# One graph layer on one core: first stage worked tile by tile, neighbour sums dealt out over other steps, feed-forward stage in another order

## What is computed

```
xn = layernorm(x)
# graph part: relation products, mean over the incoming edges, gate
u = xn @ root + bias
for r in range(8):
    sums = segment_sum(xn[src] * (edge_type == r), dst)
    u = u + (sums / max(count, 1)) @ weight[r]
z = concatenate([u, xn]) @ w_gate + b_gate
gnn = tanh(u) * z + xn * (1 - z)
# mix part: rms norm, q, k, v of 8 heads of 16, Taylor attention, w_out
x = x + gnn + mix(xn)
# feed-forward part: FP4 quantize-dequantize of rows and weights, 352 hidden
x = x + fp4_linear(silu(fp4_linear(ln(x), w_gate)) * fp4_linear(ln(x), w_up), w_down)
```

## Time and profile before

| | us |
|---|---|
| median of 3 runs | 1644.76 (1642.74 to 1646.51) |
| the profiled execution, its own time | 1644.54 |
| its span in the trace | 1642.8 |
| PE busy | 1554.4 |
| DVE, POOL, ACT busy | 890.7, 809.8, 406.0 |

### The profile page before, as it was taken

One profiled execution on the slowest core, in us unless ns is written; L12 is line 12 of the kernel. 1 busy time (PEld: TensorE's weight loads), 2 busy tenths in 40 slices (PEclk: granted clock), 3 DMA queues, 4 the chain that ended last, 5 costly groups with the idle time before them and its releaser, 6 DMA issues.

```text
span 1642.8 us, 19045 instructions
## 1 busy us (share of the span) xinstructions
PE 1554.4 (95%) x7138; PEld 1259.3 (77%) x7138; DVE 890.7 (54%) x1334; ACT 406.0 (25%) x595; POOL 809.8 (49%) x682
## 2 busy tenths in 40 slices
PE   4999999999999999999999999999999879997988
PEld 4987777777778678888887888888777758876887
DVE  6535222444442320003888888884667656877785
ACT  3321112222222112122222222222211123232320
POOL 4426766667663136545555565654655634232220
PEclk9999999999999999999999999999999989998999
DMA  4422323333333222226777788877889874540001
GB/s 160 144 89 80 92 79 94 108 98 102 95 90 112 71 78 99 84 88 222 263 254 255 245 276 281 278 242 240 301 285 317 287 257 163 186 148 0 39 39 49
DMA packets 120459, 262.48 MB, mean 160 GB/s; under 512 B 23451, under 2 KB 37010, under 8 KB 120360
## 3 DMA queue, kind: packets, MB, share of 16 engines
q1 hardware_dynamic: 48568, 109.34, 19.9%
q0 software_dynamic: 33056, 83.02, 16.6%
q10 hardware_dynamic: 38736, 68.83, 11.3%
HBM read 193.33 MB, written 80.06 MB: 166 GB/s over the span
## 4 chain that ended last, share of the span: by engine, by line
PE 63%; DVE 16%; issue 8%; DMA 6%; POOL 3%; ACT 2%; ACTq 0%; POOLq 0%; SPq 0%; DVEq 0%
PE ps L1831 49%; DMA source_rows<-relation_rows,row_list 6%; PE ps L2074 5%; PE ps L2083 2%; DVE u_sum L1580 2%; PE ps L1958 1%; PE ps L1914 1%; PE ps L1938 1%; PE ps L1950 1%; POOL source_rows L922 1%; POOL xf L1025 1%; DVE u_sum L1590 1%; ACT source_rows_hi L2292 1%; PE ps L2144 1%; DVE xf L1726 1%
## 5 line engine op out<-in xcount | busy, mean ns | idle before, releaser
L1831 PE MATMUL ps<-WH,XTH 128*128 128x512 f32 (+1 forms) x1680 | 666.9, 397 | 0.0
L1831 PE MATMUL ps<-WH,XTL 128*128 128x512 f32 (+1 forms) x1680 | 652.6, 388 | 0.0
L1831 PE MATMUL ps<-WL,XTH 128*128 128x512 f32 (+1 forms) x1680 | 652.5, 388 | 0.0
L864 POOL TENSOR_TENSOR WL<-RAW,WH 128x512 fp32r<-128x512 f32 (+1 forms) x184 | 243.6, 1327 | 289.4 <-ACT WH L2210 286.4
L1831 PEld LDWEIGHTS ps<-WH,XTH 128*128 128x128 f32 x1680 | 318.4, 190 | 65.6 <-issue 7.1
L1831 PEld LDWEIGHTS ps<-WH,XTL 128*128 128x128 f32 x1680 | 316.7, 189 | 64.8
L1831 PEld LDWEIGHTS ps<-WL,XTH 128*128 128x128 f32 x1680 | 317.6, 189 | 60.7 <-issue 2.4
L922 POOL DMA_INDIRECT source_rows<-relation_rows,row_list x180 | 221.6, 1231 | 235.4 <-DVE u_sum L1580 130.7
L2232 ACT ACTIVATE EV<-ps 128x512 f32<-128x512 f32 x180 | 107.6, 598 | 631.6 <-PE ps L1831 543.2
L943 POOL DMA_INDIRECT edge_lists<-edge_words x160 | 196.9, 1231 | 46.4 <-issue 44.2
L1580 DVE SCALAR_TENSOR_TENSOR u_sum<-source_rows,weight_list,u_sum 128x1024 f32<-128x1024 f32 x120 | 165.4, 1378 | 60.8 <-DMA source_rows<-relation_rows,row_list 55.7
(11 more groups left out here) (312 smaller groups left out, 1499.9 us busy)
## 6 DMA issues: line engine op xcount, KB each, us to landing
relation_rows<-EV ACTq DMA_DIRECT2D x160, 256.0 KB
RAW<-in_L_gnn_weight SPq DMA_DIRECT2D x128, 256.0 KB
u_rows<-u_sum SPq DMA_DIRECT2D x20, 512.0 KB
RAW<-in_L_gnn_w_gate SPq DMA_DIRECT2D x32, 256.0 KB
mix_rows<-mix_rows_out ACTq DMA_DIRECT2D x10, 512.0 KB, 2.6
root_rows<-EV ACTq DMA_DIRECT2D x20, 256.0 KB
u_sum<-u_rows SPq DMA_DIRECT2D x10, 512.0 KB
bias_rows<-root_rows SPq DMA_DIRECT2D x10, 512.0 KB, 6.5
```

Of the source, the lines that this page charges most:

```text
L864: g.tensor_tensor(WL[:, h % 2, k, 0:w], RAW[:, q % 4, 0:w], WH[:, h % 2, k, 0:w].bitcast(F32), ALU.subtract).then_inc(w_lo, 1)
L1831: mm = t_.matmul(ps[:, bank, 0:w], a[:, t, k, :], b[:, s, k, 0:w], start=(k == 0 and j == 0), stop=(k == KT - 1 and j == 2))
```

## The change

1. First stage: the statistics are handed over for one tile at a time for the first four tiles and then for pairs (`LN_TILES`); POOL's `row_scales` gives the scale and the shift first (the first of two counts of `ln_rstd`) and the norms after; the normalization moves from DVE to ACT (`norm_x`, one Identity instruction with scale and bias); the first weight's rows are scaled and rounded in one ACT instruction instead of two, their low part is made on DVE (`first_low`) instead of POOL, and the last four of the eight have buffers of their own (`RAW4`), so that all eight are loaded ahead of tile 2. Only tiles 0 and 1 are transposed ahead of the products; tile n + 1 is transposed within product n (`TRANSPOSE_AT`). POOL writes its constants ahead of the scales of tile 2.
2. Sums: group 0 starts at step 113 instead of 117, group 1 at 178 as before and ends at step 208 instead of 210. The step loops of ACT and DVE end before the last store and the last evacuation, which come after the rounds' branch on ACT and after `finish` on DVE.
3. Gate: the transposes of tile 1 come ahead of the first matmuls of tile 0.
4. Feed-forward: the weight blocks 6 to 9 are spread over `gate_up(1)`; in a loop pass DVE does `xf_round` ahead of `hidden`, and ACT does `silu(t)` ahead of `magic(t + 2)` and `norm_xf(t + 3)`; DVE's `gate_sums` of tiles 8 and 9 move back.

```diff
+
+LN_TILES = ((0, 1), (1, 2), (2, 3), (3, 4), (4, 6), (6, 8), (8, 10))
+TRANSPOSE_AT = (0, 3, 1, 1, 1, 1, 1, 1, 1)
...
-AGG_FROM = (117, 178, NSTEP)
+AGG_FROM = (113, 178, NSTEP - 2)
...
+        RAW4, = stage_tensors(("w_rows_first", [P, 4, HW], F32))
...
-            return XS[:, t + 2 if t < 4 else t - 4, :]
+            return XS[:, t if t < 6 else t - 4, :]
...
+        def raw(q):
+            return RAW[:, q % 4, 0:w_cols(q // KT)] if q < 4 or q >= KT else RAW4[:, q % 4, 0:w_cols(0)]
...
-            return (2, 4, 0)[n % 3] if n < 6 else (0, 6)[n % 2]
+            return (2, 4, 0)[n % 3] if n < 6 else (6, 6, 0, 6)[n - 6]
...
-                    sp.wait_ge(xt_ps, t - 5)
+                    sp.wait_ge(xt_ps, t - 3)
...
+                if q >= KT:
+                    sp.wait_ge(w_lo, q - 3)
...
+                    landed = raw_in[q] if q < 4 else raw_first
+                    sp.dma_start(raw(q)[:, 0:HID], w_q[k * P:(k + 1) * P, :]).then_inc(landed, 16)
+                    sp.dma_start(raw(q)[:, HID:3 * HID], w_kv[k * P:(k + 1) * P, :]).then_inc(landed, 16)
...
+            for q in range(KT):
                 load_raw(q)
             load_x(2)
             load_x(3)
...
+            load_raw(KT)
             load_x(6)
-            load_raw(4)
-            load_raw(5)
+            load_raw(KT + 1)
+            load_raw(KT + 2)
             load_x(7)
-            load_raw(6)
-            load_raw(7)
+            load_raw(KT + 3)
             load_x(8)
+            load_raw(KT + 4)
+            load_raw(KT + 5)
             load_x(9)
-            raw_next = KT
+            raw_next = KT + 6
...
+                a, b = LN_TILES[n]
+                tiles, many = slice(a, b), slice(0, b - a)
+                pool.wait_ge(ln_stats, b)
+                lch.step(g.tensor_scalar(rstd[:, tiles], mv1[:, tiles, 1], EPS, None, ALU.add))
+                lch.step(g.tensor_tensor(rstd[:, tiles], rstd[:, tiles], half_powers[:, 0, many], ALU.pow))
+                lch.step(g.tensor_tensor(shift[:, tiles], mv1[:, tiles, 0], rstd[:, tiles], ALU.mult))
+                g.tensor_scalar(shift[:, tiles], shift[:, tiles], -1.0, None, ALU.mult).then_inc(ln_rstd, 1)
+                lch.step(g.tensor_scalar(norms[:, tiles], mv1[:, tiles, 1], float(D), None, ALU.mult))
+                lch.step(g.tensor_tensor(norms[:, tiles], norms[:, tiles], half_powers[:, 1, many], ALU.pow))
+                lch.step(g.tensor_tensor(norms[:, tiles], norms[:, tiles], rstd[:, tiles], ALU.mult))
+                g.tensor_scalar(norms[:, tiles], norms[:, tiles], 1e-12, 1.0 / float(D) ** 0.5, ALU.max,
                                 ALU.mult).then_inc(ln_rstd, 1)
...
             row_scales(0)
-            for q in range(2):
-                low_rows(q)
             row_scales(1)
...
+            row_scales(2)
+            row_scales(3)
+            low_rows(KT)
+            row_scales(4)
+            low_rows(KT + 1)
+            low_rows(KT + 2)
+            row_scales(5)
+            low_rows(KT + 3)
+            pool.wait_ge(xt_ps, 6)
+            pool.wait_ge(ln_rstd, 2 * len(LN_TILES) - 2)
+            pool.wait_ge(w_lo, KT + 4)
+            g.memset(xs(NT - 1)[96:P, :], 0.0).then_inc(padded, 1)
+            pool.wait_ge(padded, 1)
+            row_scales(6)
...
-                if 1 <= t <= KT and n < NSTEP:
+                if 1 <= t <= KT and 4 < n < NSTEP:
                     low_rows(KT * (h + 1) + t - 1)
...
-            second_rstd(3, slice(NT - 2, NT))
             scaled(2)
             for t in range(2, NT):
                 rescaled(t)
                 if t + 1 < NT:
                     scaled(t + 1)
+                if t == 2:
+                    second_rstd(3, slice(NT - 2, NT))
...
+            def first_low(q):
+                dve.wait_ge(w_hi, q + 1)
+                v.scalar_tensor_tensor(WL[:, 0, q, 0:3 * HID], raw(q), gam[:, q:q + 1],
+                                       WH[:, 0, q, 0:3 * HID].bitcast(F32), ALU.mult,
+                                       ALU.subtract).then_inc(w_lo, 1)
+
+            def row_norms(n):
+                tiles = slice(*LN_TILES[n])
+                dve.wait_ge(ln_rstd, 2 * n + 2)
+                v.reciprocal(qkv_scale[:, tiles], norms[:, tiles])
+
+            def lo_x(t):
+                if t in [a for a, b in LN_TILES]:
+                    row_norms([a for a, b in LN_TILES].index(t))
+                dve.wait_ge(xth_ready, t + 1)
+                v.tensor_tensor(XTL[:, t], two_banks(2 * (t % 2)), XTH[:, t].bitcast(F32),
+                                ALU.subtract).then_inc(xtl_ready, 1)
 
             row_stats(0)
-            normed_rows(0)
             row_stats(1)
-            normed_rows(1)
+            for q in range(4):
+                first_low(q)
+            lo_x(0)
+            for q in range(4, 6):
+                first_low(q)
             row_stats(2)
-            lo_x(0)
-            normed_rows(2)
+            for q in range(6, KT):
+                first_low(q)
             lo_x(1)
             row_stats(3)
-            normed_rows(3)
             lo_x(2)
             row_stats(4)
-            normed_rows(4)
+            row_stats(5)
             lo_x(3)
+            row_stats(6)
             lo_x(4)
+            row_stats(7)
+            lo_x(5)
+            row_stats(8)
+            lo_x(6)
+            row_stats(9)
+            for t in range(7, NT):
+                lo_x(t)
...
-            for n in range(min(AGG_FROM[0], QUANT_FROM) - 1, NSTEP + 1):
+            for n in range(min(AGG_FROM[0], QUANT_FROM) - 1, NSTEP):
...
             finish(NBK - 1)
+            evacuate_gate(NSTEP - 1)
...
             lo_weights(range(0, 6))
-            gate_sums(NT - 2)
             xf_round(1)
             gate_products(NT - 1)
+            xf_begin(2)
+            gate_sums(NT - 2)
+            lo_weights([6])
+            lo_xf(1)
+            hidden(0)
+            lo_weights([7, 8])
+            xf_round(2)
+            lo_weights([9])
+            lo_hidden(0)
+            xf_begin(3)
             gate_sums(NT - 1)
             second_stats(range(NT - 2, NT)).then_inc(mv2_ready, 1)
-            lo_weights(range(6, len(NAT_TILES)))
-            xf_begin(2)
-            lo_xf(1)
-            for t in range(1, NT):
-                hidden(t - 1)
+            lo_xf(2)
+            for t in range(2, NT):
                 if t + 1 < NT:
                     xf_round(t + 1)
-                if t >= 2:
-                    residual(t - 2)
+                hidden(t - 1)
+                residual(t - 2)
                 if t + 2 < NT:
                     xf_begin(t + 2)
                 lo_hidden(t - 1)
...
+                if 1 <= n < NT - 1 and k == TRANSPOSE_AT[n]:
+                    transpose_x(n + 1)
...
-                if n + 2 < NT:
-                    transpose_x(n + 2)
                 product(n, beside)
-            for m in AGGREGATES_AT[NSTEP]:
-                aggregate(m)
...
             transpose_u(0)
-            gate_high(0, 0)
             transpose_u(1)
-            gate_low(0, 0)
+            gate_half(0, 0)
             gate_half(1, 0)
...
-            transpose_weights(range(6, len(NAT_TILES)))
+            transpose_weights([6])
+            transpose_xf(1, 1)
+            gate_up(1, 1, lambda n: transpose_weights([7 + n]))
+            transpose_weights([9])
+            transpose_h(0, 0)
             pe.wait_ge(wt_lo, len(NAT_TILES))
-            transpose_xf(1, 1)
-            for t in range(1, NT - 1):
+            down(0, 0)
+            transpose_xf(2, 0)
+            for t in range(2, NT - 1):
...
-                    a.activation(raw, raw, ACT.Copy, scale=gam[:, k:k + 1]).then_inc(gam_done, 1)
-                    act.wait_ge(gam_done, k + 1)
-                need(act, prod, NT * (h - 1))
-                a.activation(WH[:, h % 2, k, 0:w], raw, ACT.Copy).then_inc(w_hi, 1)
+                    a.activation(WH[:, 0, k, 0:w], raw(q), ACT.Copy, scale=gam[:, k:k + 1]).then_inc(w_hi, 1)
+                else:
+                    a.activation(WH[:, h % 2, k, 0:w], raw(q), ACT.Copy).then_inc(w_hi, 1)
+
+            def norm_x(t):
+                n = max(n for n, (a, b) in enumerate(LN_TILES) if t >= a)
+                act.wait_ge(ln_rstd, 2 * n + 1)
+                a.activation(xs(t), xs(t), ACT.Identity, scale=rstd[:, t:t + 1],
+                             bias=shift[:, t:t + 1]).then_inc(xn_ready, 1)
...
-            for q in range(4):
+            for q in range(2):
                 hi_row(q)
+            norm_x(0)
+            for q in range(2, 4):
+                hi_row(q)
+            norm_x(1)
             hi_x(0)
-            for q in range(4, 6):
+            for q in range(4, KT):
                 hi_row(q)
             hi_x(1)
-            for q in range(6, KT):
-                hi_row(q)
-            hi_x(2)
-            for n in range(NSTEP + 1):
+            norm_x(2)
+            for n in range(NSTEP):
```

(15 more changed lines are left out.)

88 lines of the change are left out of this document (28 added, 60 removed).

## The result

The changed kernel takes 1603.64 us (1601.57 to 1604.29), the kernel before 1644.95 beside it: ratio 0.9748, 95% interval 0.9734 to 0.9762, a gain of 41.3 us where 24.3 were predicted.

A forecast was written before the change was run, and what follows sets the result against it. PE, busy 1554.4 of 1642.8 us, was taken as the bound, so gains come from its idle time or lower-clock time. Terms -13.3 - 1 + 2 - 12 = -24.3 gave 1620 us, range 1608 to 1634.

The forecast's parts named there:

- First stage: Stage up to step 10: product 0 starts at 14.9 instead of 28.07; -13.3 us in all, from -15 to -9.
- Feed-forward passes: Feed-forward loop: a pass falls from 15.08 to 14.4 us, with POOL's `rescaled` holding up DVE's `hidden`; -3.2 us.
- head: Start of the feed-forward stage: `gate_up(3)` at 1519.5 instead of 1528.15, -8.7 us; head and passes together -12.
- Sums, group 1, and the tail: Group 1's last steps to the gate: +6.4 - 3.0 - 1.4 = +2 us, from -5 to +9.
- So the gathers set the pace, not the steps: Group 1: gathers, not PE's steps, were taken to explain a tile's 22.05 us where PE needs 18.3.
- Dealing the same 70 items over 30 steps doesn't quicken that: Group 1: fewer steps keep the items' pace; the last product ends 8.4 us later, 2 given back, +6.4.
- a tile of group 1 at 20 to 22: Sign for the forecast in group 1: 20 to 22 us a tile; below 17 the gathers weren't the pace.
- Waits for the over items' low part at 25 us or more: Sign for the forecast in the sums: PE's waits for over items' low parts reach at least 25 us.
- The rival in which the gathers keep step: DVE isn't held up and gathers keep pace: feed-forward -18, group 1 and tail -2, 1610 us; chance 0.2.
- the wait of 4.40 ... stays on PE: Tail behind the last product: PE's 4.40 us wait, put down to the rounds' branch, remains.
- Sums, group 0: Group 0's 110 items over 65 steps instead of 61 can save PE waits: -1 us, between -3 and +2.

The follow-up runs named there:

- e5: Changed kernel with POOL's `rescaled` treating only half of each row's blocks in the feed-forward stage, the rest left out: 1597.12 us.
- e6: Changed kernel with `residual` ahead of `hidden` on DVE in the steady feed-forward passes, all work kept: 1600.92 us.
- e1: Changed kernel with group 1's items dealt over 32 steps again, the last over item aggregated behind the loop: 1614.44 us.
- e2: Changed kernel with group 1's 70 items dealt over 22 steps instead of 30: 1644.2 us.
- e8: Changed kernel with group 1 started at step 176 instead of 178, same end, so 32 steps: 1606.04 us, ratio 0.9739 to the kernel before.
- e11: Changed kernel with group 1 dealt over 31 steps, the last over item aggregated in the last product: 1610.45 us.
- e3: Changed kernel with group 0 started at step 117 again instead of 113: 1608.37 us.
- e10: Changed kernel with PE's old tail order, the first gate half's high part ahead of tile 1's transposes: 1607.67 us.
- e14: Changed kernel run again without any edit: 1603.4 us.
- e16: Changed kernel with `residual` ahead of `hidden`, tile 8's `gate_sums` ahead of `xf_begin(2)`, and group 1's next sum loaded one item sooner: 1593.53 us.
- e7: Kernel with group 1 over 22 steps, each gather fetching only 64 of its 128 rows: 1635.27 us.
- e13: Changed kernel with POOL issuing a step's gathers ahead of its weight row from step 178 on: 1627.1 us.
- e4: Changed kernel with the old feed-forward order on DVE, ACT, PE and POOL: 1616.23 us.
- e9: Changed kernel with a ring of three source tiles for the gathers instead of four, all work kept: 1644.72 us.
- e12: Kernel with group 1 over 22 steps, POOL issuing a step's gathers ahead of its weight row from step 178 on: 1666.79 us.

## Why the prediction was wrong

**"First stage", -13.3: right.** Product 0 at 15.60, and from there to step 10 0.3 us less than before, where 0.1 less was forecast: -12.8 in all. No run undoes this part by itself.

**"Feed-forward passes" and "head", -12: right**, by its own steps. The head gave -9.4 (from `gate_up(0)` to `gate_up(3)` 47.64 instead of 57.08) against -8.7. A pass took 14.44 against 14.4; the last, forecast at 13.3, took 14.45 too, so the six gave -1.8 against -3.2. Another 1.6 came behind `gate_up(9)`, where nothing was forecast. That the sum of -12 fits to 0.8 is in part luck: the misses cancel. The hold-up by POOL, which was read off one row, is now shown: taken away in two ways (e5, e6) it gives back 0.85 a pass. The Trainium skill, page "SBUF — State Buffer", section "SBUF: two separate sides", says that VectorE and GpSimd take a shared port pair as an exclusive lock, against VectorE instructions in a two-port mode or with two SBUF inputs. The traces agree: `residual`, which has one operand in PSUM, took 1.22 beside POOL, and `gate_sums`, which has two in SBUF, 3.06. On who starts first, which the prediction took from the page, they agree less well: by the records that `gate_sums` began 0.04 us ahead of POOL's instruction (1447.64 against 1447.68) and was the one held up. Whether the small tensor_scalar runs in such a mode, no trace shows.

**"Sums, group 1, and the tail": "So the gathers set the pace, not the steps"; "Dealing the same 70 items over 30 steps doesn't quicken that". This is the step that failed**, with 10.7 us. The sum kept the items' old pace (+8.4 for the two steps behind the last item) and gave back 2, with 10.9 as the most. Nine tiles took 13.0 us less (194.2 to 181.2), so what came back was the whole of the two steps that PE needed less, and 2 more; measured from step 180, the last low part was ready 12.9 sooner than at the old pace. e1, the same items back over 32 steps, takes 21.5 us a tile and 10.8 us more time. The slip was to take PE's waits beside a tile of 22.05 for proof of a pace that the dealing can't change. PE's need for the mean tile was 3.2 steps, 19.3 us, and fell to 18.3; the tile fell from 21.6 to 20.1. Only further down does the items' own pace show: with 2.2 steps PE needs 13.9, and the tile is 19.9 (e2).

By steps to a tile the runs gave: 3.2, 21.6 and 21.5 (before, e1), but 20.3 in e8 without its one long tile; 3.1, 21.3 (e11); 3.0, 20.1 to 20.6 (changed, e3 to e6, e10, e14 to e16); 2.2, 19.9 (e2). So it isn't the number of steps alone: before, e1 and e11 have the last item at the end or one step from it, e8 two steps from it. Why that should count for all tiles isn't shown.

The prediction's own sign was too blunt: "a tile of group 1 at 20 to 22" came true with 20.1, but over nine tiles that span is 18 us, more than the term. "Waits for the over items' low part at 25 us or more" was wrong: they were 10 to 14. The rival in which the gathers keep step had this sign with -2 for group 1 and the tail together; it was -13.

**The tail, "the wait of 4.40 ... stays on PE": wrong.** It was 0.6 to 3.9 in the runs that aggregate nothing behind the last product (1.39 and 1.57 in the changed kernel) and 4.26 in e1. It went with how long the last weight row had been done: in the eight profiles in which POOL's last `low_rows` ended 4.7 us or more ahead of PE's last product or aggregation (the kernel before, e1, e2, e7, e10 to e13) it was 3.1 to 4.4, in the ten in which it ended 4.0 us or less ahead (the changed kernel among them) 0.6 to 2.4. No run tells whether one causes the other, so this part of the gain is found, not explained. The step rightly had ACT's branch out of the way and tile 1's transposes in the gap, but both at the lower clock; with gaps of 1.4 and 0.4 instead of 4.4 and 4.0 PE never fell, so transposes and gate ran at 2.4 GHz. That a short gap is enough isn't shown: behind 2.42 in e5 the clock fell, behind 3.59 in e11 it didn't. Predicted -4.4, measured -8.7.

**"Sums, group 0", -1: right in its mechanism, too small.** The forecast priced the wait alone, and not in full. The wait of 2.95 went, and with it what followed it: in the kernel before, PE's timeline behind it was

```profile
880.39 0.73 PE L1958 MATMUL ps<-source_rows_hi,edge_one_hots 128*128 128x512 f32 x2 [2.95 <-DVE source_rows_lo L1564]
880.96 0.86 PE L1958 MATMUL ps<-source_rows_lo,edge_one_hots 128*128 128x512 f32 x2
881.62 0.63 PE L1831 MATMUL ps<-WH,XTH 128*128 128x512 f32 x1
882.05 0.63 PE L1831 MATMUL ps<-WL,XTH 128*128 128x512 f32 x1
```

with matmuls every 0.43 us until 884.18, at 1.2 GHz. Measured -4.4 in steps 10 to 179; e3 puts the start at 3.4 us in its stretch and 4.7 of the time.

**Do the parts add up?** Undone one at a time, the end of group 1 with the tail (e1) is worth 10.8, the start of group 0 (e3) 4.7 and the feed-forward order (e4) 12.6; with the first stage's 12.8 that is 40.9 of 41.3. There is little interplay between them.

**What stays open:** what holds the items at 19.9 us a tile with 22 steps. It isn't the bytes (e7). The ring has a part (e9), and the waits of e13 show one for SP's queue with 30 steps; a fifth slot wasn't tried, and e12 can't settle POOL's order. Open too is what sets PE's gap ahead of the first transposes, 0.6 to 4.4 us.

## What to carry to other kernels

That one engine waits in a stage doesn't show that the other side has a fixed pace: here a need 1 us shorter made the tile 1.5 us shorter. Change the need alone and look at the pace (as e2 does) before you price an edit by it. Price a wait with what follows it: the wait of 2.95 us on PE cost some 1.5 us more at the lower clock, and e2's 25.4 us of further waits cost 12.8 more, though some waits of the same length cost nothing more. Where an engine's queue frees buffers for another's, moving an instruction is a change on both: ask who waits for what it releases.

## What the runs showed of the hardware

- PE's clock fell behind single waits of 2.95 (half-speed matmuls until 3.8 us after it) and 3.31 us, and in the kernel before behind one of 2.10 at 1317.11. It didn't fall behind waits of 2.81 (e14, at 1196.19), 3.00 (e6, at 1239.29) and 3.59 (e11). In e2, with eleven waits, it stood at 0.84 to 0.86 over stretches of 20 and 27 us.
- A DVE tensor_scalar of 22 columns took 0.18 us alone and 1.04 beside a POOL tensor_tensor that had begun 0.94 us before it, ending with it in all seven passes. In the other direction, POOL's instruction at 1443.31 took 2.92 instead of 1.94 beside a DVE instruction with two SBUF inputs that had begun 0.16 us sooner.
- Gathers of half the rows hardly quickened the items: 19.6 us a tile against 19.9.
